# One attention stage of a fused eleven-stage kernel, rewritten: two sequences in 128 rows, masks added by matmul in the score bank, eight pairs in flight

## What is computed

```python
h = h + _L1_ffn_ref(_layernorm(h, axis=-1), ...)
...
def _L1_ffn_ref(x, ln1_w, ln2_w, wq, wk, wv, wo, router_w, w1, w2, w3):
    NH, NKV, HD, NE, TOPK = 4, 2, 16, 8, 2
    h = _rmsnorm(x, ln1_w)
    q, k, v = h @ wq.T, h @ wk.T, h @ wv.T           # 4, 2 and 2 heads of 16
    q = q * cos + _rotate_half(q) * sin              # the same for k
    scores = einsum('bhtd,bhsd->bhts', q, k) / sqrt(16)
    scores = where(causal, scores, -1e30)
    y = softmax(scores) @ v
    x = x + y @ wo.T
    flat = _rmsnorm(x, ln2_w)
    probs = softmax(flat @ router_w.T)               # 8 experts, the best two kept
    weights = the two best probs, divided by their sum + 1e-9, at their experts
    out = sum over e of weights[:, e] * (silu(flat @ w1[e].T) * (flat @ w3[e].T)) @ w2[e].T
    return x + out
```

## Time and profile before

| | us |
|---|---|
| median of 3 runs | 9736.86 (9732.4 to 9858.74) |
| the profiled execution, its time | 9755.44 |
| the profiled execution, its span | 9753.6 |
| TensorE matmul busy in the span | 8114.1 (83%) |
| mean granted TensorE clock, share of 2.4 GHz | 0.674 |

### The profile page before, as it was taken

How to read it: one execution, slowest core, us unless ns; L and a number is a source line. 1 busy time by engine, 2 the same in 40 slices (tenths; PEclk the granted TensorE clock), 3 DMA queues, 4 the chain that set the end, 5 groups by cost and what they waited for, 6 DMA issues and landing times. The chain is left out here.

```text
span 9753.6 us, 133122 instructions
## 1 busy us (share of the span) xinstructions
PE 8114.1 (83%) x40361; PEld 5958.8 (61%) x40361; DVE 4793.1 (49%) x11789; ACT 2652.9 (27%) x6187; POOL 794.8 (8%) x804
## 2 busy tenths in 40 slices
PE   4399567988778778798999787888888898878888
PEld 4266454546556555565777555777777777756666
DVE  1455344545555555344444565455555455545555
ACT  3234100001111111243222113444444444423333
POOL 0022111000000000121000000000000000000000
PEclk9977555555555555798555555677777677769999
DMA  0100111111111111332000110000000000000000
GB/s 8 26 21 21 26 40 34 24 24 9 9 9 10 9 9 9 61 81 58 15 15 15 23 27 15 5 5 5 5 5 5 5 3 5 5 15 13 11 11 10
DMA packets 637014, 172.15 MB, mean 18 GB/s; under 512 B 612740, under 2 KB 632244, under 8 KB 636726
## 3 DMA queue, kind: packets, MB, share of 16 engines
q1 hardware_dynamic: 636854, 170.45, 10.0%
HBM read 124.98 MB, written 45.40 MB: 17 GB/s over the span
## 5 line engine op out<-in xcount | busy, mean ns | idle before, releaser
L2951 DVE TENSOR_TENSOR att_SM<-att_pS,att_mask 125x498 f32<-125x498 f32 x512 | 346.1, 676 | 952.3 <-PE att_pS L2768 889.1
L2768 PE MATMUL att_pS<-att_kT,att_qT 64*125 64x249 f32 x2048 | 749.0, 534 | 0.9 <-ACT att_V L2848 0.9
L2797 PEld LDWEIGHTS att_pO<-att_V,att_PTr 124*125 124x125 f32 (+1 forms) x4096 | 700.4, 248 | 64.9 <-issue 22.0
L2797 PE MATMUL att_pO<-att_V,att_PTr 124*125 124x64 f32 (+1 forms) x4096 | 670.4, 322 | 0.0
L2782 PE MATMUL att_pP<-att_ident,att_P 124*125 124x124 f32 (+1 forms) x2048 | 484.2, 375 | 187.9 <-ACT att_P L2866 187.9
L2782 PEld LDWEIGHTS att_pP<-att_ident,att_P 124*125 124x125 f32 (+1 forms) x2048 | 364.9, 253 | 421.4 <-issue 421.4
L2866 ACT ACTIVATE att_P<-att_SM,att_nb 125x249 f32<-125x249 f32 x1024 | 503.2, 494 | 359.6 <-DVE att_nb L2953 359.6
L2859 ACT ACTIVATE att_PTr<-att_pP 125x498 f32<-125x498 f32 x512 | 300.0, 586 | 927.9 <-PE att_pP L2782 927.9
L2768 PEld LDWEIGHTS att_pS<-att_kT,att_qT 64*125 64x125 f32 x2048 | 435.3, 254 | 108.2 <-issue 20.4
L3095 PEld LDWEIGHTS sw_pY<-sw_w,sw_hT 128*125 128x125 f32 x4096 | 466.1, 189 | 3.7
L3095 PE MATMUL sw_pY<-sw_w,sw_hT 128*125 128x64 f32 x4096 | 461.4, 271 | 0.0
(11 more groups left out here) (512 smaller groups left out, 16742.5 us busy)
## 6 DMA issues: line engine op xcount, KB each, us to landing
moe_share<-mixing SPq DMA_DIRECT2D x64, 498.0 KB
att_F<-h_stream SPq DMA_DIRECT2D x192, 62.5 KB
att_X<-h_stream SPq DMA_DIRECT2D x192, 62.5 KB
ffn_w<-in_w1b SPq DMA_DIRECT2D x128, 32.5 KB
ffn_w<-in_L_ffn_W SPq DMA_DIRECT2D x128, 32.0 KB
h_stream<-att_H SPq DMA_DIRECT2D x64, 62.5 KB
ffn_F<-h_stream SPq DMA_DIRECT2D x64, 62.5 KB
ffn_X<-h_stream SPq DMA_DIRECT2D x64, 62.5 KB
```

The lines of the kernel that those rows point to most:

```text
L2768: ins = pe.matmul(pS[:, s % 2, t * T:t * T + T], qT[r:r + D, u, hp, b, t * OFF:t * OFF + PT], kT[r:r + D, u, hp, b, :], start=True, stop=True,
L2797: ins = pe.matmul(pO[:, t, hd * D:(hd + 1) * D], PTr[0:ROWS[kt], s % 2, kt, t * OFF:t * OFF + PT], V[0:ROWS[kt], u, 2 * kt + b, hd * D:(hd ...
L2951: link(v.tensor_tensor(SM[:, s % 2, :, :], pS[:, s % 2, 0:2 * T].rearrange("p (t n) -> p t n", t=2), mask[:, u, b:4:2, :], ALU.add))
```

## The change

`stage_attention1` is rewritten on `waves`, with eight parts (pre, proj, front, main, post, ends, last, mixed; so up to eight pairs are in work) and loop bodies of four slots (`PERIOD`). In it:

- both sequences of a pair share 128 rows: transposes take 128 columns at once, projections run in two halves, `wo`, `wv` and the router are block-diagonal;
- the causal masks are kept in bf16 and written into the score bank by a matmul of the 125-row bf16 identity by 374 mask columns, before the scores of that head are accumulated on top; VectorE takes maxima and ScalarE exponentiates straight from the bank;
- each step has the key scores of one pair and the query scores of the next;
- the values are stationary, the exponentials move (249 and 125 columns), the result is turned by four transposes;
- the two norms share one centering and one sum of squares (`HalfNorm`, `ways=2`), the weights `ln1`, `ln2` are ScalarE scales of the copies that follow the transposes, and much of the normalising, both rotary additions and the residual move to GpSimd;
- ranks are taken from differences compared with a table of ties; the weights are transposed on TensorE and stored as 16 rows of 249 elements;
- `flat` is stored as [128, 249] per pair, and moe1 loads it by one DMA where it had two.

```diff
 def waves(engine, parts, steps, period=2):
...
-                parts[k](n, (u - k) % 2, step)
+                parts[k](n, (u - k) % period, step)
...
+    STEPS, PERIOD, WAVES = 8, 4, 12
...
+                def project(k, n, u):
+                    for j in range(2):
+                        for b in range(2):
+                            r = slice(b * C, (b + 1) * C)
+                            ins = pe.matmul(pQ[:, b, j * T:(j + 1) * T], wqk[r, 2 * k + j, :], xT[r, u % 2, :],
+                                            start=True, stop=True)
...
+                def proj(n, u, step):
+                    if step == 1:
...
+                        turned_rows(pO, xg[:, :, :, :].rearrange("p t b c -> p t (b c)")).then_inc(*xT_done.one())
+                    if step == 2:
...
+                        project(0, n, u)
+                    if step == 4:
...
+                        project(1, n, u)
...
+                def by_query(n, u, s):
+                    b, r = s // H, 32 * (s % H)
+                    bank = pS[:, 2 + s % 2, :]
...
+                    pe.wait_ge(*max_ready.after(n, s - 2))
+                    pe.matmul(bank[:, 0:LOW], ident16[0:PT, 0:PT], mask16[:, 0, :], start=True, stop=True)
+                    pe.matmul(bank[:, 0:PT], qT[r:r + D, u % 2, b, 0:PT], kT[r:r + D, u, b, 0:PT], start=False,
+                              stop=True, tile_position=(r, 0), skip_group_check=True)
+                    pe.matmul(bank[:, PT:LOW], qT[r:r + D, u % 2, b, OFF:T], kT[r:r + D, u, b, :], start=False,
+                              stop=True, tile_position=(r, 0), skip_group_check=True).then_inc(*s_done.one())
...
+                def by_key(n, u, s):
+                    b, r = s // H, 32 * ((s + 2) % H)
+                    bank = pS[:, s % 2, :]
+                    if s % H == 0:
+                        pe.wait_ge(*qm_ready.after(n, b))
+                    pe.wait_ge(*exp_ready.after(n, s - 2))
+                    pe.matmul(bank[:, 0:LOW], ident16[0:PT, 0:PT], mask16[:, 1, :], start=True, stop=True)
+                    pe.matmul(bank[:, 0:T], kT[r:r + DV, u, b, 0:PT], qmT[r:r + DV, b, :], start=False, stop=True,
+                              tile_position=(r, 0), skip_group_check=True)
+                    pe.matmul(bank[:, T:LOW], kT[r:r + DV, u, b, OFF:T], qmT[r:r + DV, b, OFF:T], start=False,
+                              stop=True, tile_position=(r, 0), skip_group_check=True).then_inc(*st_done.one())
...
+                def main(n, u, step):
+                    if step == 0:
...
+                        turn_max(n, 1)
+                    by_key(n, u, step)
...
+                def post(n, u, step):
+                    if step == 0:
...
+                        for b in range(2):
+                            for hd in range(H):
+                                pe.matmul(pO[32 * hd:32 * hd + 32, b * T:(b + 1) * T],
+                                          V[0:OFF, u % 2, 0, b * KV + hd // 2, :], EX[0:OFF, u % 2, b, hd, 0:T],
+                                          start=True, stop=True)
+                            for hd in range(H):
+                                ins = pe.matmul(pO[32 * hd:32 * hd + 32, b * T + OFF:(b + 1) * T],
+                                                V[:, u % 2, 1, b * KV + hd // 2, :], EX[:, u % 2, b, hd, T:LOW],
+                                                start=False, stop=True, skip_group_check=True)
...
+                waves(pe, (nothing, proj, front, main, post, ends, last, mixed), STEPS, PERIOD)
...
+                def main(n, u, step):
+                    a.wait_ge(*st_done.after(n, step))
+                    a.activation(EX[:, u % 2, step // H, (step + 2) % H, :], pS[:, step % 2, 0:LOW], ACT.Exp,
+                                 scale=D ** -0.5).then_inc(*exp_ready.one())
...
+                    v.wait_ge(*s_done.after(n, step))
+                    v.tensor_reduce(M[:, 0, b, hd, D:DV], bank[:, 0:PT], AX.X, ALU.max, negate=True)
+                    v.tensor_reduce(M[:, 1, b, hd, D:DV], bank[:, PT:LOW], AX.X, ALU.max, negate=True).then_inc(
+                        *max_ready.one())
```

More of the change, by code:

```diff
@@ L580, with __init__ @@
 class HalfNorm:
-    def __init__(self, st, bodies, name="norm", rows=PT, groups=4):
+    def __init__(self, st, bodies, name="norm", rows=PT, groups=4, ways=1, about=True):
         self.sum = st.sb(name + "_sum", [rows, groups])
@@ L650, in slot @@
                     continue
-                parts[k](n, (u - k) % 2, step)
[L652 to L656, removed]
+                parts[k](n, (u - k) % period, step)
+    whole = (PAIRS - depth + 1) // period
     for s in range(depth - 1):
-        slot(s, s % 2)
+        slot(s, s % period)
     with engine.Fori(0, whole) as j:
[L660 to L663, removed]
+        for u in range(period):
+            slot(j * period + (depth - 1 + u), (depth - 1 + u) % period)
+    for s in range(depth - 1 + period * whole, PAIRS + depth - 1):
+        slot(s, s % period)
 def since(n, first):
@@ L1732, in hand_on, with store @@
+                def store(n, u):
+                    sp.wait_ge(*h_ready.after(n))
+                    st.held(sp)
+                    for ins in store_pair(sp, hx_dram, H1[:, u, :, :, :], n):
+                        ins.then_inc(*stored.one(u))
                     sp.wait_ge(*flT_ready.after(n))
@@ L1760, in _, with last @@
+                def last(n, u, step):
+                    if step == 3:
+                        w = lg[:, :, :]
+                        other, own = bcm(w, 2, E), bc(w, E)
+                        g.wait_ge(*l_exp.after(n))
+                        g.wait_ge(*rank_ready.before(n))
+                        g.tensor_tensor(over[:, :, :, :], other, own, ALU.subtract).then_inc(*compared.one())
+                waves(g, (pre, proj, nothing, nothing, nothing, ends, last, nothing), STEPS, PERIOD)
             @block.tensor
@@ new lines, in post, with ends @@
+                    if step == 6:
+                        pe.wait_ge(*oT_ready.after(n))
+                        st.held(pe)
+                        for t in range(2):
+                            ins = pe.matmul(pX[0:PT, t * 2 * C:(t + 1) * 2 * C], oT[:, t * OFF:t * OFF + PT], wo[:, :],
+                                            start=True, stop=True)
+                        ins.then_inc(*y_done.one())
+                def ends(n, u, step):
+                    if step == 5:
+                        pe.wait_ge(*fl_ready.after(n))
+                        pe.wait_ge(*flT_ready.before(n))
+                        pe.wait_ge(*OT_ready.after(upto(n + 1)))
+                        pe.wait_ge(*xT_ready.after(upto(n + 4)))
+                        if since(n, 2):
+                            pe.wait_ge(*mixT_ready.after(n - 2))
+                        st.held(pe)
+                        turned_rows(pO, fl[:, :, :].rearrange("p (t b) c -> p t (b c)", t=2)).then_inc(*flT_done.one())
@@ new lines, in last @@
+                def last(n, u, step):
+                    if step == 1:
+                        pe.wait_ge(*flT_ready.after(n))
+                        pe.wait_ge(*l_shifted.before(n))
+                        pe.wait_ge(*x2_ready.after(upto(n + 1)))
+                        st.held(pe)
+                        for t in range(2):
+                            ins = pe.matmul(pX[0:PT, t * 2 * E:(t + 1) * 2 * E], flT[:, u % 2, t * OFF:t * OFF + PT],
+                                            wr[:, :], start=True, stop=True)
+                        ins.then_inc(*l_done.one())
@@ L2021, in split_weights @@
+                waves(v, (pre, proj, front, main, post, ends, last, nothing), STEPS, PERIOD)
 def split_weights(v, w, rest, hm, mh, lh, chain):
```

731 lines of the change are left out of this document (400 added, 331 removed).

## The result

The changed kernel takes 9368.31 us (median of four runs, 9321.96 to 9384.81), the kernel before 9751.08 (four runs as well). The ratio, of the means of these runs, is 0.9578, with a 95% interval of 0.9499 to 0.9656: faster, and 39 us above the 9329 forecast. The profiled run took 9362.64 us, where 9347 was forecast from the profiled run before.

The account below looks back on a forecast made before the run. att1 was taken as bound by TensorE at the lower clock plus about 11 us of chain per pair. 32 x 43.5 + 45 = 1437 us for the stage, 408 less, gave 9329 us in all, range 8960 to 9440.

Parts of the forecast that it names:

- Bound and period: att1: TensorE at the lower clock bounds it; 43.5 us a pair, 32 pairs plus 45 us of edges, 1437 us.
- The score group: att1, one head's scores by key or query with mask: 1.96 us (1.86 to 2.14), 16 per pair, 31.4 us.
- The passage: Switch between 16-row tiles and the whole array for a mask: taken at 0.10 us, bounded at 0 and 0.28.
- No overlap across a mask: att1 steps: whole-array masks keep key and query scores apart, so a step takes 3.92 us, not 2.38.
- The rest of TensorE: Per pair at the lower clock, projections, values, transposes, output projection, value projection and router logits: 14.4 us.
- The 5% taken off: Same prices on att0 gave 19.1 us against 18.2 measured, so 45.8 us a pair was cut to 43.5.
- The other engines: Per pair in att1: VectorE some 14 us, ScalarE 8, GpSimd 9 (up to 12), all beside TensorE's 43.5.
- The share of VectorE: Sign that the forecast is right: VectorE under 35% busy in the new att1.
- Edges and the rest of the kernel: att1's start and end: 45 us idle (30 to 70); last weights store to moe1 6 us; moe1 gains 0.
- Rivals: Clock rises (0.16), scores overlap (0.11), dear tile changes make it slower (0.03), waves stall (0.06); the forecast itself 0.64.
- rival 2: att1 steps: key and query scores overlap despite the masks; 31.7 us a pair, total 8951; chance 0.11.
- rival 1: att1: TensorE's clock goes up; at 0.73, 29.8 us a pair, total 8891; at 0.60, 9098; chance 0.16.

Follow-up runs that it names:

- x4: Changed kernel with each mask matmul written twice; 9388.6 us, ratio 0.9632 to the kernel before.
- x9: Changed kernel with both masks of a step first, but key and query scores put in the same rows of the array; 9219.0 us.
- x1: Changed kernel without att1's causal mask: both mask matmuls of each step removed; 8790.5 us.
- x2: Changed kernel with both masks of a step first, then key and query scores next to each other; 8705.8 us.
- x8: Changed kernel with the masks first in each step and each mask matmul written twice; 8657.5 us.
- x3: Changed kernel with the masks added by VectorE again and none on TensorE; 8724.6 us.
- x10: Changed kernel with masks first, and masks and scores ahead of values, transposes and output projection in each step; 8722.6 us.
- x7: Changed kernel with masks first and the projections of k moved from step 4 to step 7, right ahead of the values; 8736.7 us.

## Why the prediction was right

- **Bound and period.** Forecast 43.5 us a pair and 45 us idle, 1437 in sum; by that accounting it was 1406.9 / 32 = 44.0 and 34.2, 1441. Right, with small errors against each other.
- **The score group.** 1.96 forecast, 4.03 / 2 = 2.02 measured, inside 1.86 to 2.14. The stream of 0.32 was right (0.31, x4). The passage beside it, taken at 0.10, was 0.14 and, by query, 0.19. That the 1.54 us from the earlier trace rows hold passages too, as the forecast had it, x9 bears out: with none between them both kinds take 2.79 us (2818.61 - 2815.82), 1.40 each.
- **No overlap across a mask.** Right, and shown by x1 and x2, which take the mask from between and have the overlap. The forecast priced this only as a rival; mending the order is worth more (660 us, x2) than the whole change gained (383 us between the medians). The Trainium skill, TensorEngine Tiling (Array Packing), section Key Properties, has it that changing the tiling mode drains TensorE. x9 agrees, at an estimated 0.24 us per change. The same section of the Trainium skill has it that different tiles can work in parallel. The 0.01 us between the starts in x1 agree.
- **The rest of TensorE.** Forecast 14.4 us; read from the timeline at the lower level it is about 13: values 2.66, projections 1.96 twice, output projection 1.01, and transposes, value projection and logits 5.4 (forecast 6.7). So at the lower level a pair is 8 x 4.03 + 13 = 45.2 us, and the slots without a spell measure 45.13; before the 5% the forecast had 45.8.
- **The 5% taken off.** Its reason was wrong, and that its size came out right was luck. The forecast called the method too high, but the method was right to 1.5% (45.8 against 45.13). Of the 2.2 us from there to the mean of 42.92, 1.2 are the spells at the upper level (13 x 2.9 us over 31 slots), 0.7 the short last slot, and the rest the first slots and the last but one. Mean clock 0.52, as forecast.
- **The other engines.** VectorE 12.6 (14), ScalarE 7.0 (8), GpSimd 8.2 us (9); the wider power took 1.65 us against 1.02, under twice. From 2250 to 3550 us TensorE waited for none of them. Right. The share of VectorE, 29%, is under the 35% named as a sign.
- **Edges and the rest of the kernel.** The stage fell by 403.6 us where 408 were forecast. From the last store of weights to moe1's first load it took 3.9 us (6 forecast). Behind the stage 14.5 us were given back, and ahead of it 3.9 gained: 393 in the profiled runs. moe1 is no faster for its one DMA less, as forecast: from its first load to the start of GpSimd's last multiplication it took 561.5 us before and 562.7 after. So some 13 of the 14.5 lie in stages that the change doesn't touch (last section).
- **Rivals.** None of them came in the changed kernel. But rival 2 (the overlap, 31.7 us) and rival 1 (the clock) both came when the order was mended: x2 would be at about 32 us by the overlap alone, and is at 21.0 with the clock. The Trainium skill, TensorE: Matmul & The Clock Gate, Part 1, has it that activity releases the throttle. By busy time that did not hold here: TensorE had no gap in the changed kernel and stayed at 0.52. x4 and x8, where only masks were added, show that it matters what the matmuls are.

## What to carry to other kernels

A small whole-array matmul between matmuls of few rows costs far more than its stream when it separates two that could pass together: here 2.48 us a step for two of 0.31. Group such matmuls ahead of the ones in different rows of the array, which then pass together: masks first takes 8706 us (x2), against 9368 for the change as made and 9751 before. Or leave the masks to an engine that has room: with VectorE adding them it is 8725 us (x3). And read the granted clock with each edit: a TensorE that is 100% busy at 0.52 isn't at its limit.

## What the runs showed of the hardware that was not expected

Added work cost little or nothing: with two masks instead of one per score group the period went from 21.04 to 20.82 us, and the clock from 0.86 to 0.98; without overlap it went from 42.92 to 44.30 where the masks' own time is 5.0, and the clock from 0.52 to 0.57. The same matmuls in another order gave 0.86, 0.80 or 0.73 (x2, x10, x7), and what decides is open.

The unchanged stages behind att1 take from 5690 (x3) to 5826 us (x2), from moe1's first load to the end. The difference lies behind moe1 and goes with the clock there. Windows from 2000 us behind moe1's first load to the end, of x2 and of x3:

```profile
4878.14:8703.70 3825.56, 3379.45 (x17765) 2593.52 (x17764) 1981.68 (x4745) 1518.58 (x3789) 205.60 (x248) 0.77 0.03 7
```

```profile
5061.27:8751.00 3689.73, 3264.43 (x17766) 2507.86 (x17765) 1980.57 (x4745) 1519.02 (x3789) 205.67 (x248) 0.80 0.03 7
```

The instructions are the same to one or two, VectorE's and ScalarE's busy time too, and 136 us lie between them. Why the clock differs there is open. So a total doesn't rank two versions of att1 that are less than some 140 us apart; the period says more.
